# Attention of a language-model block: which engine normalises the rows of the next group

## What is computed

```
h   = table[x] + lora_A.T[x] @ lora_B.T            # embedding
xn  = (h - mean(h)) / sqrt(var(h) + 1e-5)          # the rows that the change is about
cq, ckv = layernorm(xn @ W_dq), layernorm(xn @ W_dkv)   # 128 wide each, with gain and bias
Q = cq @ W_uq;  K, V = halves of ckv @ W_ukv       # 16 heads of 32
h   = h + concat_heads(softmax(causal(Q K^T / sqrt(32))) V) @ W_o.T
h   = h + ffn(layernorm(h))                        # shared expert + 16 routed experts
```

## Time and profile before

| what | value |
|---|---|
| timed, median of 3 | 2489.7 us |
| profiled execution | 2494.01 us, span 2492.2 us |
| PE busy | 2366.0 us (95%) |
| ACT busy | 1863.0 us (75%) |
| DVE busy | 1786.4 us (72%) |
| POOL busy | 1179.5 us (47%) |

### The profile page before, as it was taken

The page is one execution under the profiler, slowest core; times in us unless marked ns, Lnnn a source line. Parts: engine busy times, 40 slices in busy tenths (PEclk is TensorE's granted clock), DMA queues, the critical chain, the costliest instruction groups (busy, mean ns, idle before and its releaser), DMA issues.

```text
span 2492.2 us, 47182 instructions
## 1 busy us (share of the span) xinstructions
PE 2366.0 (95%) x13379; PEld 1857.0 (75%) x13380; DVE 1786.4 (72%) x3651; ACT 1863.0 (75%) x4624; POOL 1179.5 (47%) x1333
## 2 busy tenths in 40 slices
PE   3799999999999999999999999999999999999998
PEld 2577667776777766688888888888888888888887
DVE  5788888888888885856656656656656656657655
ACT  1688888888888897867767767767767767767766
POOL 3454455555454442534534544544544544545544
PEclk9899999999999999999999999999999999999999
DMA  3222222222222223331321321321321321321322
GB/s 109 59 80 70 74 82 70 72 77 72 79 83 81 73 69 103 123 107 43 106 89 42 106 89 42 106 88 43 106 89 42 106 88 43 106 87 44 105 72 60
DMA packets 99829, 198.22 MB, mean 80 GB/s; under 512 B 10928, under 2 KB 10928, under 8 KB 99568
## 3 DMA queue, kind: packets, MB, share of 16 engines
q1 hardware_dynamic: 94576, 179.29, 22.1%
q0 software_dynamic: 5120, 17.31, 2.9%
HBM read 145.66 MB, written 50.86 MB: 79 GB/s over the span
## 4 chain that ended last, share of the span: by engine, by line
issue 30%; POOL 26%; PE 2%; DVE 1%; ACT 1%; POOLq 1%; DVEq 0%; ACTq 0%
POOL t_lo L1314 24%; POOL sh_lo L1314 2%; POOLq L1312 1%; DVE ps_u L1681 0%; DVE f_lo L1706 0%; DVE t L1688 0%; ACT t_hi L1533 0%; PE fwork L1329 0%; PE ps_g L1329 0%; ACT square L1516 0%; PE ps_g L1331 0%; PE ps_g L1330 0%; PE ps_u L1331 0%; PE ps_u L1329 0%; PE ps_u L1330 0%
## 5 line engine op out<-in xcount | busy, mean ns | idle before, releaser
L1314 POOL TENSOR_TENSOR t_lo<-t,t_hi 128x512 fp32r<-128x512 f32 x512 | 663.4, 1296 | 414.1 <-ACT t_hi L1533 414.0
L1681 DVE TENSOR_TENSOR ps_u<-ps_u,square 128x512 f32<-128x512 f32 x512 | 357.3, 698 | 155.2 <-ACT square L1520 140.0
L470 POOL TENSOR_TENSOR probs<-probs,inv 128x512 f32<-128x512 f32 x256 | 269.5, 1053 | 396.7 <-DVE inv L919 396.3
L1533 ACT ACTIVATE t_hi<-t 128x512 fp32r<-128x512 f32 x512 | 320.5, 626 | 111.1 <-PE ps_y L1331 65.7
L1688 DVE TENSOR_TENSOR t<-ps_u,res 128x512 f32<-128x512 f32 x512 | 354.1, 692 | 54.8 <-DVE ps_u L1681 20.5
L1516 ACT ACTIVATE square<-ps_g 128x512 f32<-128x512 f32 x544 | 320.1, 588 | 91.9 <-PE ps_g L1331 90.1
L732 ACT ACTIVATE probs<-ps_s,nmax 128x128 f32<-128x128 f32 x1024 | 368.6, 399 | 6.6 <-DVE nmax L909 3.9
L1520 ACT ACTIVATE square<-square 128x512 f32<-128x512 f32 x544 | 344.1, 633 | 17.3
L732 ACT ACTIVATION_READ_ACCUMULATOR probs<-ps_s,nmax 128x1 f32 x1024 | 244.4, 239 | 0.0
L1314 POOL TENSOR_TENSOR sh_lo<-t,sh_hi 128x512 fp32r<-128x512 f32 x32 | 42.0, 1313 | 389.6 <-ACT sh_hi L1533 389.6
L743 ACT ACTIVATE pT<-ps_t 128x512 f32<-128x512 f32 x256 | 158.8, 620 | 89.9 <-PE ps_t L625 88.7
(11 more groups left out here) (197 smaller groups left out, 5510.1 us busy)
## 6 DMA issues: line engine op xcount, KB each, us to landing
res<-w_rows SPq DMA_DIRECT2D x256, 256.0 KB, 3.2
h<-rows SPq DMA_DIRECT2D x64, 256.0 KB, 2.0
res<-h SPq DMA_DIRECT2D x64, 256.0 KB, 4.0
h<-res SPq DMA_DIRECT2D x64, 256.0 KB, 2.0
rows<-h SPq DMA_DIRECT2D x16, 1024.0 KB, 5.6
keep<-h SPq DMA_DIRECT2D x16, 1024.0 KB, 7.3
out<-keep SPq DMA_DIRECT2D x64, 256.0 KB, 2.3
keep<-in_w_ffn SPq DMA_DIRECT2D x12, 512.0 KB, 3.8
```

What stands on the lines that cost most here:

```text
L470: pool.tensor_tensor(probs[:, s % RING, :, :], probs[:, s % RING, :, :], inv[:, s % RING, :].rearrange("p (h o) -> p h o", o=1).to_broadca ...
L1314: pool.tensor_tensor(lo, t[:, t_slot(j), :], hi.bitcast(F32), ALU.subtract).then_inc(t_lo_done, 1)
L1533: act.activation(dst, t[:, t_slot(j), :], ACT.Copy).then_inc(t_hi_done, 1)
L1681: dve.tensor_tensor(dst, product, square[:, j % 2, :], ALU.mult).then_inc(t1_done, 1)
```

## The change

POOL normalises the rows of group n+2 instead of DVE. The four instructions are the same and stand in the same step of the turn (`NORM_AT`, 10), on POOL behind the products of slot 9, the copy of the indices and the first gather. The Newton root that they read is POOL's own, so they wait for its semaphore there. Two waits are added on DVE, since `h` and the root's buffer are no longer protected by DVE's own order: `h_add` (L815) waits until the normalisation of the group before has read `h`, and `c_seed` until it has read the root.

```diff
             # gpsimd
+            def normalise(g):
+                pool.wait_ge(newton, 2 * NEWTON_OPS * g + NEWTON_OPS)
+                for t in range(TILES):
+                    pool.tensor_scalar(xn[:, t, :], h[:, t, :], moments[:, t, 0:1], nw[:, 4, t:t + 1],
+                                       ALU.subtract, ALU.mult).then_inc(xn_done, 1)
...
                     if step == RSTD_AT and has_part(n, "xt", 0):
                         newton_of(2 * NEWTON_OPS * (n + 2), TILES)
+                    if step == NORM_AT and has_part(n, "xt", 0):
+                        normalise(n + 2)
             # vector
             def h_add(n, t):
                 full(dve, n, "h", t)
                 at_least(dve, res_kept[t], 16 * (n + 2))
+                at_least(dve, xn_done, TILES * (n + 2))
...
             def c_seed(g):
                 dve.wait_ge(c_moments, 2 * TILES * (g + 1))
+                dve.wait_ge(xn_done, TILES * (g + 1))
...
-            def normalise(g):
-                dve.wait_ge(newton, 2 * NEWTON_OPS * g + NEWTON_OPS)
-                for t in range(TILES):
-                    dve.tensor_scalar(xn[:, t, :], h[:, t, :], moments[:, t, 0:1], nw[:, 4, t:t + 1],
-                                      ALU.subtract, ALU.mult).then_inc(xn_done, 1)
...
-                        if step == NORM_AT:
-                            normalise(n + 2)
```

## The result

The changed kernel takes 2568.66 us (median of 4 runs, 2567.67 to 2570.51) against 2495.69 us of the kernel before, timed beside it (a fourth run, of 2501.69 us, has come to the three of before): a ratio of 1.0297, 95% interval 1.0265 to 1.0329. Forecast were 2471 us in a range of 2463 to 2505. The profiled execution has a span of 2565.8 us, 73.6 us more than before.

What follows compares the result with a forecast made beforehand. PE, busy 95% of the span, was taken as the bound, waiting at "k" 0 for DVE. 23.4 - 2.5 - 1.1 - 1.5 = 18.3 us less than 2489.7 gave 2471 us, range 2463 to 2505.

Steps and rivals of the forecast that it cites:

- The bound: PE at "k" 0 waits for DVE's addition L903, delayed by normalising; 1.67 us a turn would go, 23.4 in 14.
- The price d: Time of one 128x512 normalisation on POOL, not in the trace; guessed 0.70 us, between 0.633 and 1.62.
- The loss per turn, 4d - 2.92: PE's added waits at "xt" 0 and slot 10 together, in us a turn, once one normalisation exceeds 0.73 us.
- turn -2: Early turn, normalisations behind the clearing of `k_diag`: last done at 39.05 instead of 36.52, 2.5 us lost at most.
- turn 0: Turn without "out": PE waits 1.1 us longer for POOL's product of slot 10.
- turn -1: Early turn: two tiles are done when PE, held by another copy, reaches the second; no loss.
- the waits: Issue cost of the waits added on DVE: taken as 0.1 us a turn, 1.5 us in 15 turns.
- (b): Rival: POOL bounds steps 10 to 13, slower; 2512 us at 1.34 us an instruction, 2531 at 1.62; chance 0.20.
- (c): Rival: gathers land too late, PE waits 0.7 us at "art" in 13 turns; 2480 us; chance 0.10.
- (a): Rival: the wait changes its place, to "xt" 0 and slot 10, at 1.05 us an instruction; 2492 us; chance 0.17.

Runs made afterwards that it cites:

- the copy: The changed kernel with POOL's four normalisations replaced by plain copies of h to xn, mean and root left out: 2464.69 us, ratio 0.9884 to the kernel before.
- v1: The kernel before, normalisation on DVE, with tiles 0 and 1 moved one step earlier, to step 9: 2469.15 us, ratio 0.9872 to the kernel before.
- v2: The kernel before, normalisation on DVE, with all four tiles in step 9, ahead of the readout of "ct": 2472.23 us, ratio 0.9882 to the kernel before.

## Why the prediction was wrong

**The bound**: right. The wait at "k" 0 was the normalisation's, and it went, in the changed kernel as with the copy. It was worth more than its idle time of 1.67 us: the copy's turn is 1.95 us shorter. Some 0.15 us of that is in how idle time is counted: with the copy, "k" 0 starts 0.23 us behind the last matmul of "q" 0 (391.15 to 391.38); before, it started 2.05 us behind it (396.11 to 398.16), which is 1.82 us more. The idle time runs only from that matmul's shown end, 0.39 us after its start. Where the last 0.13 us come from stays open. In some turns the wait cost more than that, which the rows of one turn could not tell: in three turns of the profile before, the granted clock fell behind this wait, and turns of 57.4 to 58.0 us are the result. The first line is a steady turn from "k" 0 on, the second one of the three:

```profile
398.10:403.10 5.00, 4.94 (x42) 3.68 (x43) 4.45 (x8) 2.29 (x6) 2.28 (x3) 1.00 0.59 159
623.64:628.64 5.00, 4.94 (x36) 3.58 (x36) 4.06 (x7) 1.19 (x2) 2.29 (x3) 0.69 0.53 159
```

From turn 1 on, no turn of the copy, of v1 or of v2 has such a fall.

**The price d**: this step failed, the sentence "I take 0.70, next to the 0.633". It measured 2.075. The row that I called the least trustworthy, 11 ns for four more columns of the same instruction, was the nearest: drawn out it gave 1.62, and exactly that form measured 1.504. The 0.633 us was another operation with one input, on bf16, and so is a copy with 0.612; this form costs two and a half times that. What is alike in inputs and outputs was not alike in price. And even 1.62 was no upper end: it came from a form with one operation and a constant, while the kernel's has two operations and two scalars from SBUF, 0.57 us more. A bound by the nearest row holds only as far as the row has the same work in it.

What the Trainium skill says of one-input elementwise work on GpSimd, roughly line rate (GPSIMD Engine Reference, section 4.1, Engine selection), fits here the copy alone, 0.612 us, and not this form, 2.075. That of section 8, Key points, that VectorE is about twice as fast, errs on the same side: the same instruction on VectorE took 0.53 us at the shortest, a quarter. The measurements decide.

**The loss per turn, 4d - 2.92**: right as a term. With the measured d it gives 5.38 us; PE's two waits are 1.30 + 3.68 = 4.98, and with 1.04 us they are 0.46 + 0.27 = 0.73 a steady turn where 1.25 was worked out. Part of what was left out is that POOL comes to the block sooner: without DVE's instructions beside them its two low parts take 2.54 us, not 2.72. With d = 2.075 the whole sum of the prediction would have read: 14 x (5.38 - 1.67) = 51.9, turn -2 8.0, turn 0 6.6, turn -1 about 3, the waits 1.5: some 71 us. The span shows 73.6.

**What the sum lacked**: the clock. No term stood for what PE loses after a wait. It is 1.57 us in a turn where the clock falls, which it does in 11 of the 13 turns; over these 13 the changed kernel takes 18.6 us more than the one with PE kept busy. That 71 lies so near 73.6 all the same is luck, since other terms were too large. Without the clock a turn loses 3.24 us where 5.38 - 1.67 = 3.71 stands in the sum, the first turns came to 16.5 us where 17.6 stand, the added waits to nothing that can be told, and the kernel before loses clock of its own in three turns.

**The rivals**: (b), POOL as the bound of steps 10 to 13, is what happened, at the places that the prediction named, "xt" 0 and slot 10. It had a chance of 0.20, and its upper end, 2531 us, was too low by nearly 40. (c) fell: PE waits at "art" in no steady turn, neither in the changed kernel nor with the copy, whose turn is shorter than forecast. (a)'s price was tried as such and came out better than worked out, 0.45% below the kernel before.

## What to carry to other kernels

Price an instruction that moves to another engine by the same operation on that engine, however small its rows are: here their step from size to size (1.62 us, where that form measured 1.50) said more than a large row of another operation, 0.633. Where an engine has a free stretch of known length (here 2.92 us), compare the block with it before anything else, and put a block that is longer in pieces between the products that others await. Before moving work to another engine, look whether it is slow only for its neighbours: the same four instructions on the same engine, one step earlier, gave the gain that the change was after.

## What the runs showed of the hardware that was not expected

- POOL's `tensor_scalar` on 128x512 fp32: 1.50 us with one operation and a constant, 2.075 with two operations and two scalars from SBUF, against 0.61 for a copy and 1.04 for a product with a broadcast operand.
- After an idle PE of 3.68 us the granted clock fell in 10 of 12 turns, after 3.18 us in about every second one; the stretch behind it then showed 0.63. 14 matmuls in the wait kept it at 1.00. In the kernel before it fell behind 3 of the 14 waits of 1.67 us.
- DVE's four instructions of 128x512 take 1.91 us beside an idle POOL and 4.61 us beside a busy one.
